# In the loop over states of a selective scan: one product moved from VectorE to GpSimd, one running sum moved from GpSimd to TensorE

## The reference, cut to what matters

```
dt = softplus(dt @ dt_proj_w.T + dt_proj_b)
A = -exp(A_log)
dA = exp(dt[..., None] * A)                       # 256 channels x 16 states
dBu = (dt * u)[..., None] * Bm[:, :, None, :]
h = dA_t * h + dBu_t                              # for every token t
y = einsum('lbin,bln->bli', h_seq, Cm)            # sum over the 16 states
y = (y + u * D) * silu(gate)
s = y @ out_proj_w.T

h = silu(xf @ w1[e]) * (xf @ w3[e])               # experts e = 0..3
g = silu(sum_e gates[:, e] * (h @ w2[e]))
```

## Time and profile before

| | |
|---|---|
| median of 3 runs | 5822.17 us |
| span of the profiled execution | 5822.4 us |
| median of the runs less that span | -0.2 us |
| PE busy | 4385.6 us (75%) |
| DVE busy | 4514.1 us (78%) |
| ACT busy | 2924.5 us (50%) |
| POOL busy | 2325.4 us (40%) |
| granted clock of PE, mean | 0.895 |
| one state of layer 2's loop, mean over 15 of them | 5.69 us |

### The profile page before, as it was taken

The page is one execution under the profiler, slowest core; times in us unless marked ns, Lnnn a source line. Parts: engine busy times, 40 slices in busy tenths (PEclk is TensorE's granted clock), DMA queues, the critical chain, the costliest instruction groups (busy, mean ns, idle before and its releaser), DMA issues. The chain is left out here.

```text
span 5822.4 us, 60164 instructions
## 1 busy us (share of the span) xinstructions
PE 4385.6 (75%) x16724; PEld 2482.1 (43%) x16724; DVE 4514.1 (78%) x8572; ACT 2924.5 (50%) x5085; POOL 2325.4 (40%) x1980
## 2 busy tenths in 40 slices
PE   5876778767787677876778767787678866788776
PEld 1533435344353443534435344353444524444344
DVE  3678966789657996579965799658995489955898
ACT  3544645446444564445644456444564445645455
POOL 0134631447204562045620456104661046610565
PEclk9998889978899888998889988998889998899888
DMA  2000000000000000000000000000000000000000
GB/s 99 1 1 2 1 3 1 1 2 1 3 1 0 2 1 3 1 1 2 1 3 1 2 1 1 3 1 2 1 1 3 1 2 1 1 3 1 2 1 2
DMA packets 3537, 22.97 MB, mean 4 GB/s; under 512 B 336, under 2 KB 336, under 8 KB 2640
## 3 DMA queue, kind: packets, MB, share of 16 engines
q1 hardware_dynamic: 3152, 18.59, 0.8%
HBM read 16.23 MB, written 2.36 MB: 3 GB/s over the span
## 5 line engine op out<-in xcount | busy, mean ns | idle before, releaser
L1622 POOL TENSOR_SCALAR l_pp<-l_sc,l_m 128x512 f32<-128x512 f32 x496 | 783.4, 1579 | 644.3 <-DVE l_m L1572 596.7
L1572 DVE MAX8 l_m<-l_wk 128x8 f32<-128x512 f32 x1536 | 980.6, 680 | 0.0
L224 PE MATMUL bank<-l_v,l_pt 128*128 128x99 f32 (+1 forms) x5888 | 871.4, 300 | 139.5 <-ACT l_pt L1362 114.7
L224 PEld LDWEIGHTS bank<-l_v,l_pt 128*128 128x128 f32 x5888 | 814.9, 216 | 196.7 <-ACT l_pt L1362 154.0
L1316 PE MATMUL bank<-consts,l_pp 128*128 128x128 f32 x2048 | 390.9, 323 | 526.3 <-POOL l_pp L1629 519.8
L1180 POOL TENSOR_TENSOR l_hc<-l_h,l_cn 128x1024 f32<-128x1024 f32 x128 | 302.3, 2362 | 989.0 <-DVE l_h L1130 989.0
L1316 PEld LDWEIGHTS bank<-consts,l_pp 128*128 128x128 f32 x2048 | 280.2, 165 | 959.7 <-POOL l_pp L1629 828.2
L224 PE MATMUL bank<-l_km,hold 128*128 128x512 f32 x1024 | 652.7, 727 | 43.3 <-DVE l_ol L1539 18.1
L1568 DVE MATCH_REPLACE8 l_wk<-l_m,l_wk 128x512 f32<-128x512 f32 x1024 | 684.1, 675 | 0.0
L1392 ACT ACTIVATE l_sc<-bank 128x512 f32<-128x512 f32 x512 | 303.3, 594 | 739.9 <-PE bank L224 738.5
L1629 POOL TENSOR_TENSOR l_pp<-l_pp,l_ex 128x512 f32<-128x512 f32 x496 | 631.0, 1272 | 26.4 <-ACT l_ex L1399 5.7
(11 more groups left out here) (350 smaller groups left out, 8065.6 us busy)
## 6 DMA issues: line engine op xcount, KB each, us to landing
weights<-weights_dram SPq DMA_DIRECT2D x1, 11014.0 KB, 29.0
hold<-x_dram SPq DMA_DIRECT2D x9, 256.0 KB, 2.6
out_dram<-x SPq DMA_DIRECT2D x9, 256.0 KB, 3.4
consts<-consts_dram SPq DMA_DIRECT2D x1, 1503.0 KB, 32.2
rotary<-consts_dram SPq DMA_DIRECT2D x1, 1024.0 KB, 34.1
```

The source lines that it names most:

```text
L224: return nc.tensor.matmul(o, lhsT, rhs, start=start, stop=stop)
L1572: nc.vector.max(m8[n % RM][:, k + 1], wk_[n % 2][:]).then_inc(S["top"], 1)
L1622: nc.gpsimd.tensor_scalar(pp[n % 2][:], sc[n % RS][:], m8[n % RM][:, 3, 0:1], None, ALU.is_ge).then_inc(S["kept"], 1)
```

## The change

The product with B goes from DVE to POOL. Since POOL takes B from SBUF, ACT now copies bank 2 into `bn` (two buffers: a slice of `hold` that held `y1` before, and a part of `xp`, which is free by then). POOL's program alternates: db(n), then hc(n-1) (`weigh`). The running sum `y1` on POOL is gone: PE sums the second half too, into bank 3. So C can no longer use bank 3; B and C of a state now go through bank 2 one after the other, with ACT's copy of B between them.

```diff
-                sq, rs, left, y1 = (hold[:, i] for i in range(4))
+                sq, rs, left, bn0 = (hold[:, i] for i in range(4))
...
+                bn = [bn0, xp[:, 0, 0:T]]
...
@@ -924,7 +925,8 @@
                         def gather(n):
                             pe.wait_ge(S["hc"], n + 1)
-                            mm(bank[6][:], C("ident"), hc[n % 2][:, 0], n == 0, n == NS - 1).then_inc(S["y"], 1)
+                            mm(bank[6][:], C("ident"), hc[n % 2][:, 0], n == 0, n == NS - 1)
+                            mm(bank[3][:], C("ident"), hc[n % 2][:, 1], n == 0, n == NS - 1).then_inc(S["y"], 1)
...
@@ -951,13 +953,12 @@
                             if n:
-                                pe.wait_ge(S["db"], n)
+                                pe.wait_ge(S["cn"], n)
                             mm(bank[2][:], pick[:, n:n + 1].to_broadcast([96, 128]), parts[:]).then_inc(S["Bn"], 1)
                             if n:
-                                pe.wait_ge(S["cn"], n)
-                            mm(bank[3][:], pick[:, NS + n:NS + n + 1].to_broadcast([96, 128]), parts[:]).then_inc(S["Cn"], 1)
-                            if n:
                                 w1(n)
+                            pe.wait_ge(S["bn"], n + 1)
+                            mm(bank[2][:], pick[:, NS + n:NS + n + 1].to_broadcast([96, 128]), parts[:]).then_inc(S["Cn"], 1)
                             if n >= 2:
                                 gather(n - 2)
...
@@ -1025,12 +1026,16 @@
                         for n in range(NS):
+                            a.wait_ge(S["Bn"], n + 1)
+                            if n >= 2:
+                                a.wait_ge(S["db"], n - 1)
+                            act(bn[n % 2], bank[2][:], ACT.Copy).then_inc(S["bn"], 1)
                             if n:
                                 expert(n - 1)
                             a.wait_ge(S["Cn"], n + 1)
...
-                            act(cn[n % 3][:], bank[3][:], ACT.Copy).then_inc(S["cn"], 1)
+                            act(cn[n % 3][:], bank[2][:], ACT.Copy).then_inc(S["cn"], 1)
...
@@ -1144,11 +1149,6 @@
-                            v.wait_ge(S["Bn"], n + 1)
-                            if n >= 2:
-                                v.wait_ge(S["h"], 2 * n - 2)
-                            tt(db[n % 2][:], du[:], bank[2][:, None, :].to_broadcast([128, 2, T]),
-                               ALU.mult).then_inc(S["db"], 1)
...
@@ -1156,8 +1156,7 @@
-                        v.wait_ge(S["y1"], NS - 1)
-                        for n, yn in enumerate((bank[6], y1)):
+                        for n, yn in enumerate((bank[6], bank[3])):
...
@@ -1171,22 +1170,25 @@
-                        for n in range(NS):
+                        def weigh(n):
+
                             g.wait_ge(S["h"], 2 * n + 2)
                             g.wait_ge(S["cn"], n + 1)
                             if n >= 2:
                                 g.wait_ge(S["y"], n - 1)
-                                g.wait_ge(S["y1"], n - 1)
-                            nc.gpsimd.tensor_tensor(hc[n % 2][:], hh[n % 2][:],
-                                                    cn[n % 3][:, None, :].to_broadcast([128, 2, T]),
+                            nc.gpsimd.tensor_tensor(hc[n % 2][:], hh[n % 2][:], cn[n % 3][:, None, :].to_broadcast([128, 2, T]),
                                                     ALU.mult).then_inc(S["hc"], 1)
 
+                        g.wait_ge(S["du"], 2)
+                        for n in range(NS):
+                            g.wait_ge(S["bn"], n + 1)
+                            if n >= 2:
+                                g.wait_ge(S["h"], 2 * n - 2)
+                            nc.gpsimd.tensor_tensor(db[n % 2][:], du[:], bn[n % 2][:, None, :].to_broadcast([128, 2, T]),
+                                                    ALU.mult).then_inc(S["db"], 1)
                             if n:
-                                g.wait_ge(S["hc"], n + 1)
-                                if n >= 2:
-                                    g.wait_ge(S["y1"], n - 1)
-                                nc.gpsimd.tensor_tensor(y1[:], hc[0][:, 1] if n == 1 else y1[:], hc[n % 2][:, 1],
-                                                        ALU.add).then_inc(S["y1"], 1)
+                                weigh(n - 1)
+                        weigh(NS - 1)
```

## The result

The changed kernel takes 5946.88 us (median of 4 runs, 5942.75 to 5949.36), the kernel before 5821.38 (4 runs). The ratio is 1.0217, 95% interval 1.0202 to 1.0231: slower by 126 us. The profiled execution has a span of 5944.6 us and took 5946.36; its span is 122.2 us above that of before (5822.4), so sums made from the two traces go against 122, not 126.

A forecast was written before the change was run, and what follows sets the result against it. DVE was taken to set the pace, 5.69 us a state. Loop +14.5, head +0.8 and tail +1.7 gave +17.0 us a batch, over 8 batches +136, so 5958 us; own range 5940 to 5975, 8-in-10 range 5930 to 6000.

The forecast's parts named there:

- the tail: Behind each loop: PE's second last sum, taken at the low clock, adds 1.7 us a batch.
- the head: Ahead of hc(0): scans wait for POOL's db(1), +0.8 us a batch, bounds 0 and 2.4.
- The state: One loop step: 0.08 to hc, hc 2.35, scan 1.08, POOL's db 2.14, scan 1.08; sum 6.73 us.
- y1's turn: In the loop before, POOL's y1 ran between the two scans, costing DVE 1.06 us a state.
- hc loses its cover: With db off DVE, only the expert's 1.29 us runs beside hc; DVE then waits 1.14 us.
- Who goes first: At hc's end the scan goes ahead of POOL's db; rival, POOL first in every state, 5986 us, chance 0.20.
- the gates': Every fourth state, gate work on PE and DVE makes the scan late; POOL goes first, 7.05 us.
- The margin of 0.3 us: In the loop, the scan waits by 6.42 us, 0.3 ahead of hc's end at 6.73.
- The loop: hc(0) to hc(15): 11 x 6.73 + 3 x 7.05 + 4.67 = 99.9 against 85.35, +14.5 us a batch.
- the forecast's chain: In the head: ACT copies B, PE spreads C, ACT copies C, makes da, copies state 1's B; then db(1).
- PE as the bound: Rival in the loop: low-clock PE work, 9.4 us a state, near 6250; a few states, 6000 to 6050; chance 0.08.

The follow-up runs named there:

- e9: e8 with DVE's db reading B from ACT's SBUF copy, made ahead of da; PE's spread of C waits for that copy: 5848.07 us, ratio 1.0045.
- e8: e1 with ACT's da and tanh ahead of the copy of C, and PE's w2 product behind the next B: 5746.22 us, ratio 0.9866.
- e3: The kernel before without the running sum y1 on POOL; DVE takes the last hc in its place: 5725.32 us, ratio 0.9836.
- e10: The changed kernel with ACT's tanh of state n-1 ahead of the copy of B(n): 5950.55 us, ratio 1.0224.
- e4: The changed kernel without the second sum on PE; DVE takes the last hc in its place: 5958.27 us, ratio 1.0237.
- e1: The changed kernel with db back on DVE, read from PSUM, without ACT's copy of B; PE spreads C behind the sums: 5876.47 us, ratio 1.0100.

## Why the prediction was right

The forecast was +136 us, the measurement +126 by the medians and +122 between the two traces. The mechanism and the size of a state came as forecast. The sum is off by the tail, put too high by 14 us; the head, put too low by 4, hides a part of that by luck, and so do two small errors within the loop.

- *The state.* 6.73 us forecast, 6.74 measured. The terms held one by one in the state shown: hc 2.36, from its end to that of the first scan 1.07, from there to db's end 2.15, from there to the end of the second scan 1.08, and 0.08 to the next hc. e9 against e8 shows the mechanism by itself, e3 the size of y1's turn.
- *hc loses its cover.* Held: the scans are issued 0.3 us ahead of hc's end in the state shown. In the kernel before DVE's db, with its operand in PSUM, had been hc's cover, as in e8.
- *Who goes first.* The scan, as forecast, wherever it stood ready. In five of the eight batches the pattern is that of the forecast: 6.73 to 6.75, and three longer intervals, the gates'. These are 6.95 and not 7.05; POOL's db starts 2.30 us after hc there, where the forecast had 2.38. Three batches have one or two more, four in all, and one gate's interval is 7.67, where db waits for ACT's copy of B. The two of the first batch are of this kind:

```profile
381.13 3.64 PE L224 MATMUL bank<-l_hc,consts 128*128 128x512 f32 x4 [1.96 <-POOL l_hc L1179]
...
385.46 2.34 POOL L1179 TENSOR_TENSOR l_hc<-l_h,l_cn 128x1024 f32<-128x1024 f32 x1 [1.16 <-DVE l_h L1135]
...
386.75 0.60 ACT L1032 ACTIVATE hold<-bank 128x512 f32<-128x512 f32 x1 [5.72 <-PE bank L224]
...
387.76 2.37 POOL L1187 TENSOR_TENSOR l_db<-l_du,hold 128x1024 f32<-128x1024 f32 x1
...
387.86 0.69 DVE L1141 SCALAR_TENSOR_TENSOR hold<-hold,bank 128x512 f32<-128x512 f32 x1 [2.48 <-ACT hold L1025]
...
392.41 2.35 POOL L1179 TENSOR_TENSOR l_hc<-l_h,l_cn 128x1024 f32<-128x1024 f32 x1 [2.28 <-DVE l_h L1135]
```

  PE's four instructions of the sums, issued at 381.13, took 3.64 us, against 1.98 in other states: the lower of the two clock levels, after 1.96 us of waiting for hc. (The other such state has 3.68 at 435.68.) So B came late, its copy at 386.75 (L1032) and with it the tanh; the expert began at 387.86 (2.48 us idle ahead of it), and db, started at 387.76, went first. The margin of 0.3 us was worked out at the full clock only; that was the weak point of the working. It cost 2 x 0.21 us in the first batch and nothing in most others, and 6.95 instead of 7.05 gave more than that back. e10 removed the dependence and with it all these intervals.
- *The loop.* +14.5 a batch forecast, +14.2 measured (113.3 over 8). The forecast's 99.9 for a loop meets a mean of 99.8; the first batch's 85.35, from which it counted, is 0.3 below the mean of the eight before.
- *Head.* +0.8 forecast, +1.2 to +1.4 measured in the eight batches. POOL's db(1), for which the scans wait, starts 4.65 us after `du` (353.67 against 349.02), where the forecast's chain comes to 4.0. In that chain PE ran at the lower level: the product with w3 at 350.62 takes 1.91 us against 1.02 at 362.52, and the spread of B behind it came late. As for the margin, the working had the full clock only.
- *Tail.* +1.7 forecast, -0.1 measured. This is the term that was mis-sized. Timeline of the changed kernel's end of loop:

```profile
458.31 2.34 POOL L1179 TENSOR_TENSOR l_hc<-l_h,l_cn 128x1024 f32<-128x1024 f32 x1 [2.27 <-DVE l_h L1135]
...
460.70 1.98 PE L224 MATMUL bank<-l_hc,consts 128*128 128x512 f32 x4 [2.63 <-POOL l_hc L1179]
...
462.73 1.41 DVE L1160 SCALAR_TENSOR_TENSOR l_du<-l_u,weights,bank 128x512 f32<-128x512 f32 x2 [4.50 <-PE bank L224]
```

  and busy time in two short stretches of the changed kernel, the sums of the state above and these last ones (PEclk is the column behind POOL's):

```profile
381.10:384.70 3.60, 3.57 (x5) 1.60 (x6) 3.60 (x2) 0.00 (x0) 3.20 (x1) 0.53 0.00 0
460.60:462.60 2.00, 1.90 (x5) 0.94 (x6) 0.00 (x0) 0.00 (x0) 0.05 (x1) 1.00 0.00 0
```

  The last two sums, four instructions, take 1.98 us, where before two took 2.08. I had taken the lower clock from the kernel before and forecast it for twice the work; in the changed kernel PE had begun the previous sums 4.6 us earlier, waited 2.63, and had the full clock, 1.00 against 0.53. Twice the work then costs nothing against half of it at half the clock. All eight batches have 1.98 or 1.99 here, behind waits of 0.94 to 2.63 us, while e10's have 3.38 to 3.40 in four. So the forecast's level was possible, and no run shows what decides it. The 1.8 us too much, over 8 batches, are 14 us, more than the whole error of 10; the head, 0.5 us a batch too low, took 4 back.
- *PE as the bound.* Not here (e4), but in part of e8's states, once the turns are gone.

What stays open: what sets PE's level ahead of the last sums; and by what rule the one or the other engine is let in. In the changed kernel's trace a scan and a POOL instruction of this loop meet 295 times; the one that started first by the profile also ended first each time, and the two ends are never less than 1.08 us apart. Strict turns and the order of waiting would look the same in these traces, and no run parts them.

## What to carry to other kernels

In a loop like this one, of float32 scans and products, moving an elementwise product from VectorE to GpSimd frees nothing if VectorE's other work has both inputs in SBUF: the two take turns, and their times add. Count per step the time of all GpSimd instructions and of VectorE's two-SBUF-input instructions together, and put VectorE's instructions with a PSUM operand beside GpSimd's; the sum is the floor (6.73 worked out, 6.74 measured). An operand left in PSUM can be worth more than an idle engine (102 us between e8 and e9). A sum that TensorE can accumulate is the part of this change to keep, but only with the orders of e8; e1 has it too and is slower than before. And a saving in a loop can be lost behind it: e10's 7 us went into tails in which PE ran at its lower level.

## What the runs showed of the hardware

- An engine that has its next instruction ready without a gap still lets the other in: db at 360.60 followed hc at once, and the scan, waiting since 360.33, ran ahead of it.
- The exclusion follows the operands: a DVE product with one operand in PSUM kept 1.21 to 1.22 us in all 112 cases beside hc (e8), with both in SBUF it ended 1.08 us behind hc in all 112 (e9), and took 1.22 where hc didn't run.
- An instruction that waits for its turn has part of its start behind it: POOL's db takes 2.36 us alone and 2.15 after the wait, y1 1.27 and 1.06, DVE's db 1.22 and 1.08, a scan some 1.16 and 1.08.
- Less work on PE made the kernel no faster and its mean clock lower (e4: 0.882 against 0.899), and more work at the loop's end was free, since it ran at the full clock. The length of PE's wait alone didn't tell which: 1.96 us (changed kernel) and 1.47 (e10) were followed by the low level, 0.94 and 2.63 (changed kernel) by the full one.
